# Projecting the next layer's first tile inside the last feed-forward groups, with separate buffers for W1's parts and another order in a feed-forward group (a linear-attention block, then a six-layer local-attention transformer, fp32, one core)

## Chip, cores and metric

One core of a Trainium2 chip. The metric is device time in microseconds; lower is better. Engines: TensorE (PE), VectorE (DVE), ScalarE (ACT), GpSimd (POOL), and SyncE (SP), whose queue here issues every DMA.

## What is computed

Input `x` is (4, 1024, 128). First a linear-attention block with 16 heads of 8 is added to it, then `L0_ffn`, which is itself a stack of six layers of local attention (16 heads of 64, window 32) and a gated feed-forward:

```python
x = x + _L0_attn_ref(_layernorm(x), Wq, bq, Wk, bk, Wv, bv, Wo, bo)
x = x + _L0_ffn_ref(_layernorm(x), ...)          # the six layers:
for i in range(6):
    x = attn_layer(shift_tokens(x), Wqkv[i], q_scale[i], k_scale[i], Wo[i]) + x
    x = ffn_layer(shift_tokens(x), ln_g[i], ln_b[i], W1[i], b1[i], W2[i], b2[i]) + x
# attn_layer: q, k l2-normed per head, scaled, rotary, softmax over own and previous window, @ Wo
# ffn_layer: xn = layernorm(x) * g + b; a, gate = split(xn @ W1 + b1); a * gelu(gate) @ W2 + b2
```

`shift_tokens` takes the second half of the channels from the token before. 4096 tokens are 32 tiles of 128 (`NT`), and 8 groups of 4 tiles (`NG`, `FT`) in the feed-forward.

## The kernel before

All five engines have their own instruction stream, written out by hand; they meet at semaphores (`wait_ge`, `then_inc`). Within an engine everything runs in the order of its text. For tile semaphores `done(T)` is the count after tile (or group) T.

**Attention of a layer.** `every_tile(step, depth)` runs `step(k)` for each tile as a software pipeline: step k holds the projection of tile k (`project`, three matmuls of 512 columns per half, from a high and a low part of `x` and of `Wqk`), the transposes, scores and value products of tile k-1, and the outputs of tiles k-2 and k-3. For one tile: TensorE transposes it (`xs_transposed`), ScalarE copies its high part (`xsT_upper`), DVE makes the low part (`xsT_lower`), TensorE projects `q` and later `k`; ScalarE squares them (`square`), DVE multiplies by the rotary tables (`rotate`) and makes the norms (`inverse_norms`), GpSimd adds (`add_rotated`, line 1545) and scales `k` (`normalise_k`, line 1554), TensorE transposes the results (line 595). Value and output weights are multiplied into `wvo` once per layer (`wv_transposed`, `wvo_product` on TensorE; `wvT_evacuated`, `wvo_evacuated` on ScalarE); the high and low part of `Wqk` are made by `wqk_upper` (ScalarE) and `wqk_lower` (GpSimd), in two pieces of 811 and 1237 columns.

**Feed-forward of a layer.** Eight groups. For group u, from the SP queue's `ffn_tokens(u)` (three DMAs: 128 partitions, 127 partitions, 1 partition) into one of six buffers `xs4`: DVE `centre` (lines 768, 770), ScalarE `squared4`, DVE `variance4` (line 775 on), GpSimd `group_rsqrt` (12 steps, lines 1457 to 1460), DVE `normalised` (line 785, writes `xn4`), TensorE `transpose4` (line 506), ScalarE `transposed` and `upper`, DVE `lower` (line 1111). Then TensorE `up(u, par, 0..2)` (lines 526 to 528), ScalarE `gelu`, DVE `hidden`, TensorE `down` (line 540), DVE `x_new` (line 1128) with `xb` that GpSimd's `x_and_bias` made (line 1569). Within `step4` DVE runs `hidden(u,1)`, `hidden(u,2)`, `normalised(u+2)`, `centre(u+3)`, `hidden(u+1,0)`, `variance4(u+3)`, `lower(u+2)`, `x_new(u)`. `W1`'s parts and `xnT`'s parts lie in `wqk_hi` and `wqk_lo`, which the attention no longer needs; so `w1_upper` (ScalarE) and `w1_lower` (GpSimd) run at the end of the attention, and the two pieces of the next layer's `wqk_upper` wait until the `up` of group 6 and of group 7 are through.

**SP queue.** In order: `ffn_tokens` 2 to 5, the next layer's attention weights (4 DMAs, 2 MB), `ffn_tokens` 6 and 7, the next layer's first two tiles.

**Between layers** TensorE runs, behind the last `up`: `wvo_product` 0, half of `down(7)`, `wvo_product` 1, the other half, `wvo_product` 2 and 3, then `step(0)` of the next layer. At the very end DVE adds the kept first sum (`x_keep`) for four batches and SP writes four outputs.

## Time and profile before

| | us |
|---|---|
| median of 3 runs | 3455.31 (3452.45 to 3456.94) |
| the profiled execution | 3454.96 |
| its span, first to last instruction | 3453.1 |

```profile
DVE  7788888678888668888768888877888866888876
ACT  3399998579999759999849999867999975999994
PEclk8799999999999999999999999999999999999999
```

The three lines are the span in 40 equal slices, with the busy share of VectorE and of ScalarE in tenths, and the TensorE clock that was granted, in tenths of full speed. A layer is about 550 us, 460 of them attention. In the sections below a row of a timeline is: start, length (us), engine, line, operation, output<-inputs, count, and in brackets the idle time of the engine before it with what ended it. Matmuls overlap: each is issued before the one ahead has ended. A row of a table of stages is: from:to, length, then busy time of each engine with its count of instructions, granted TensorE clock, DMA share, GB/s.

### The profile page before, as it was taken

Reading aid. Unit: us, or ns where it says so; the run is one execution under the profiler, and the core shown is the slowest. Engines: PE = TensorE matmul, PEld = TensorE weight load, DVE = VectorE, ACT = ScalarE, POOL = GpSimd, SP = SyncE. Lnnn points to the kernel's source line nnn. Section 1 sums busy time; section 2 is a strip of 40 time slices with the busy share of each in tenths; the row PEclk is TensorE's granted clock in tenths of the full one; section 3 lists DMA queues with packets and bytes.
Section 4 is the critical chain, followed back from the end, with each engine's and each line's share of the span. In section 5 each row is a group of like instructions: output and inputs, shape, how many; then the busy total and the mean of one; then the engine's idle time right before and its main releaser. Section 6 shows DMA issues by size and latency. Waiting matters only on the chain.

```text
span 3453.1 us, 114079 instructions
## 1 busy us (share of the span) xinstructions
PE 3204.9 (93%) x42076; PEld 2183.8 (63%) x42076; DVE 2797.3 (81%) x5376; ACT 2928.4 (85%) x9250; POOL 2035.8 (59%) x2150
## 2 busy tenths in 40 slices
PE   5699999889999889999889999988999988999997
PEld 4466666756666666666566666565666666666666
DVE  7788888678888668888768888877888866888876
ACT  3399998579999759999849999867999975999994
POOL 3466665456666556666556666555666655666654
PEclk8799999999999999999999999999999999999999
DMA  2000000100000100000010000010000010000002
GB/s 72 10 7 7 13 7 5 45 14 7 14 7 6 43 15 7 12 9 7 11 46 7 7 13 7 5 46 14 7 13 7 7 40 17 8 9 11 7 9 65
DMA packets 141016, 57.20 MB, mean 17 GB/s; under 512 B 118598, under 2 KB 137668, under 8 KB 139460
## 3 DMA queue, kind: packets, MB, share of 16 engines
q1 hardware_dynamic: 140484, 50.01, 6.2%
q8 instruction: 346, 5.67, 0.7%
q14 instruction: 186, 1.52, 0.1%
HBM read 22.57 MB, written 2.10 MB: 7 GB/s over the span
## 4 chain that ended last, share of the span: by engine, by line
PE 66%; DVE 11%; ACT 11%; POOL 6%; issue 5%; DVEq 0%; DMA 0%; SPq 0%; ACTq 0%; POOLq 0%
PE ring L649 16%; PE ring L595 9%; PE ring L667 7%; PE s_ps L633 7%; ACT probs L1341 6%; PE qk_ps L581 5%; PE ring L607 4%; PE qk_ps L582 4%; PE qk_ps L583 4%; PE s_ps L637 2%; DVE xn L785 2%; PE s_ps L624 2%; PE ring L540 1%; POOL qk_rot L1554 1%; POOL ln_rs L1458 1%
## 5 line engine op out<-in xcount | busy, mean ns | idle before, releaser
L1341 ACT ACTIVATE probs<-s_ps,nbias,rnorm 128x64 f32<-128x64 f32 x3072 | 1234.3, 450 | 0.4 <-DVE nbias L1060 0.4
L1545 POOL TENSOR_TENSOR qk_rot<-by_cos,by_sin 128x1024 f32<-128x1024 f32 x384 | 912.1, 2376 | 362.0 <-DVE by_sin L1010 318.9
L649 PE MATMUL ring<-wvo,xsT 128*32 128x512 f32 x6144 | 801.7, 605 | 18.1 <-ACT vo L1164 17.9
L1341 ACT ACTIVATION_READ_ACCUMULATOR probs<-s_ps,nbias,rnorm 128x1 f32 x3072 | 771.3, 251 | 0.0
L1534 POOL TENSOR_TENSOR probs<-probs,rrow 128x256 f32<-128x256 f32 x768 | 454.7, 613 | 309.6 <-DVE rrow L994 308.8
L1554 POOL TENSOR_TENSOR qk_rot<-qk_rot,rnorm 128x1024 f32<-128x1024 f32 x192 | 365.5, 1904 | 416.8 <-DVE rnorm L752 416.8
L1007 DVE TENSOR_TENSOR by_cos<-qk_ps,rotary 128x1024 f32<-128x1024 f32 x378 | 462.9, 1225 | 156.8 <-ACT squares L1327 156.4
L595 PEld LDWEIGHTS ring<-cst,qk_rot 128*128 128x128 f32 x3072 | 343.9, 141 | 279.3 <-ACT vo L1164 145.3
L595 PE MATMUL ring<-cst,qk_rot 128*128 128x128 f32 x3072 | 448.4, 279 | 75.9 <-POOL qk_rot L1545 51.7
L1022 DVE TENSOR_REDUCE sumsq<-squares 128x16 f32<-128x1024 f32 x384 | 463.2, 1206 | 0.0
L1010 DVE TENSOR_TENSOR by_sin<-qk_ps,rotary 128x1024 f32<-128x1024 f32 x378 | 459.3, 1215 | 0.0
L1327 ACT ACTIVATE squares<-qk_ps 128x1024 f32<-128x1024 f32 x378 | 399.4, 1057 | 40.0 <-PE qk_ps L583 40.0
L633 PE MATMUL s_ps<-kT,qT 128*32 128x128 f32 x10752 | 421.9, 279 | 0.0
L667 PEld LDWEIGHTS ring<-vo,pT 128*32 128x32 f32 x12288 | 344.6, 110 | 117.7 <-issue 117.7
L667 PE MATMUL ring<-vo,pT 128*32 128x128 f32 x12288 | 372.5, 273 | 5.0 <-ACT pT L1164 5.0
L1164 ACT ACTIVATE kT<-ring 64x512 f32<-64x512 f32 x576 | 339.5, 589 | 43.9 <-PE ring L595 35.1
L581 PE MATMUL qk_ps<-wqk_hi,xsT_hi 128*128 128x512 f32 x756 | 342.8, 453 | 5.2 <-DVE xsT_lo L984 5.1
L1164 ACT ACTIVATE vo<-ring 128x512 f32<-128x512 f32 x576 | 326.0, 602 | 8.2 <-PE ring L649 2.3
L633 PEld LDWEIGHTS s_ps<-kT,qT 128*32 128x32 f32 x10752 | 283.7, 109 | 60.9 <-issue 60.7
L649 PEld LDWEIGHTS ring<-wvo,xsT 128*32 128x32 f32 x6144 | 158.1, 110 | 249.3 <-ACT vo L1164 163.7
L582 PE MATMUL qk_ps<-wqk_lo,xsT_hi 128*128 128x512 f32 x756 | 304.8, 403 | 0.0
L583 PE MATMUL qk_ps<-wqk_hi,xsT_lo 128*128 128x512 f32 x756 | 304.4, 403 | 0.0
(173 smaller groups left out, 5372.8 us busy)
## 6 DMA issues: line engine op xcount, KB each, us to landing
qk_rot<-L_ffn_Wqkv SPq DMA_DIRECT2D x7, 1024.0 KB, 5.2
xs<-x_tok SPq DMA_DIRECT2D x194, 32.0 KB
xs<-x_tok SPq DMA_DIRECT2D x194, 31.8 KB
wv<-L_ffn_Wqkv SPq DMA_DIRECT2D x7, 512.0 KB, 6.8
wo_pad<-L_ffn_Wo SPq DMA_DIRECT2D x14, 256.0 KB, 7.8
xs<-x_tok SPq DMA_DIRECT2D x194, 0.2 KB
xs_first<-x_tok SPq DMA_DIRECT2D x24, 128.0 KB
by_cos<-x_tok SPq DMA_DIRECT2D x24, 128.0 KB
```

Of the source, the lines that this page charges most:

```text
L581: mm(half, xsT_hi[:, a, :], wqk_hi[:, cols], start=True, stop=False)
L595: last = nc.tensor.transpose(r[:, p * P:(p + 1) * P], qk_rot[:, 1 if qk == "k" else 0, c:c + P], ident)
L633: last = mm(sc, q, keys[:, :, c:c + 2 * WIN], start=False, stop=True, skip_group_check=True)
L649: last = mm(r[WIN * mh:WIN * (mh + 1), :], xsT[:, a, WIN * w:WIN * (w + 1)], wvo[:, mh, :, :], start=True, stop=True)
L667: last = mm(r[WIN * w:WIN * (w + 1), 0:C], pT[:, quad, side, WIN * w:WIN * (w + 1)], vo[:, at_w, quad * C:(quad + 1) * C], start=(n == 0), ...
L1007: v.tensor_tensor(heads(by_cos[:, n, :]), heads(projection_banks(qk, k, s)), table.unsqueeze(1).broadcast_to([P, H, D]), ALU.mult)
L1010: last = v.tensor_tensor(halves(by_sin[:, n, :])[:, :, ::-1, :], halves(projection_banks(qk, k, s)), table.rearrange("p (x j) -> p x j", x ...
L1022: v.tensor_reduce(sumsq[:, n * H:(n + 1) * H], heads(squares[:, n * INNER:(n + 1) * INNER]), AX, ALU.add).then_inc(summed[qk], 1)
L1164: return nc.scalar.activation(out_, in_, ACT.Copy)
L1341: last = nc.scalar.activation(probs[:, a, h // 4, :, h % 4, :], s_ps[:, half, c:c + 2 * WIN].rearrange("p (s c) -> p s c", s=2), ACT.Exp, ...
L1534: last = g.tensor_tensor(p, p, r, ALU.mult)
L1545: g.tensor_tensor(qk_rot[:, n, :], by_cos[:, n, :], by_sin[:, n, :], ALU.add).then_inc(added[qk], 1)
```

## The change

- `W1`'s two parts get buffers `w1_hi` and `w1_lo` of their own. `w1_upper` moves from behind the attention to ahead of ScalarE's step NT-6, `w1_lower` from ahead of GpSimd's step NT to ahead of NT-4.
- `xs4`'s first two buffers now lie in `hid`. Group 6 uses the buffer of group 2, group 7 that of group 3; group 6 is fetched ahead of the next layer's weights, group 7 still behind them.
- In `step4` DVE runs `centre(u+3)` ahead of `normalised(u+2)` and `variance4(u+3)` ahead of `hidden(u+1,0)`; ScalarE runs `squared4(u+3)` ahead of `gelu(u+1,0)`. GpSimd waits for `xn` of group u+2 before `x_and_bias(u)`, for u = 0 to 3.
- The tile-0 work of layers 1 to 5 moves into the layer before: transpose and `q` projection ahead of `down(7)`, the `k` projection between `wvo_product` 1 and 2, with the ScalarE and DVE parts that belong to it. `down(7)` is no longer cut by `wvo_product`. `wqk_upper` and `wqk_lower` now take two pieces of 1024 columns, the first of them during the groups. `wvo_product` uses banks 2, 3, 2, 3.
- The last layer no longer prepares weights for a layer that doesn't come. Three of the four final sums go to GpSimd, in its last groups.

The diff, cut to its changed lines (indentation reduced):

```diff
@@ -148,6 +148,7 @@
 w1 = sb("w1", [P, W1_COLS])
+w1_hi, w1_lo = [sb(name, [P, W1_COLS], F32R) for name in ("w1_hi", "w1_lo")]
@@ -178,7 +179,6 @@
 xn4 = sb("xn4", [P, FT, C])
-xs4_first = sb("xs4_first", [P, 2, FT * C])
@@ -187,13 +187,12 @@
 xs4_late = by_cos[:, :, :].rearrange("p a (b n) -> p (a b) n", b=2)
-xs4 = [(xs4_first[:, i, :] if i < 2 else xs4_late[:, i - 2, :]).rearrange("p (t c) -> p t c", t=FT) for i in range(6)]
+xs4 = [(hid[:, i + 1, :] if i < 2 else xs4_late[:, i - 2, :]).rearrange("p (t c) -> p t c", t=FT) for i in range(6)]
...
-late = 2 * INNER - W1_COLS - FT * P
-w1_hi, w1_lo = [parts[:, late:late + W1_COLS] for parts in (wqk_hi, wqk_lo)]
-xnT_hi, xnT_lo = [[parts[:, c:c + FT * P] for c in (late - FT * P, late + W1_COLS)]
+late = INNER
+xnT_hi, xnT_lo = [[parts[:, c:c + FT * P] for c in (late, late + FT * P)]
@@ -284,9 +283,11 @@
 def xs4_buffer(u):
-    return u % 6
...
-wvo_banks = (0, 0, 2, 3)
+    return u if u < 6 else u - 4
...
+def wvo_bank(r, layer):
...
+    return (2, 3, 2, 3)[r] if layer else (0, 0, 2, 3)[r]
@@ -385,7 +386,7 @@
         for p in (2 * r, 2 * r + 1):
-            last = mm(ring[:, wvo_banks[r], (p % 2) * 2 * C:(p % 2 + 1) * 2 * C], wvT[:, p, :], wo_pad[:, p, :, :],
+            last = mm(ring[:, wvo_bank(r, layer), (p % 2) * 2 * C:(p % 2 + 1) * 2 * C], wvT[:, p, :], wo_pad[:, p, :, :],
@@ -478,6 +479,7 @@
         pe.wait_ge(wq_ready, 2 * l + 2)
+        last_layer = l == DEPTH - 1
@@ -669,6 +671,17 @@
                 last.then_inc(o_ps, 1)
+            if only == "queries":
+                xs_transposed(0)
+                project("q", 0, 0)
+                project("q", 1, 0)
+                return
+            if only == "keys":
+                project("k", 0, 0)
+                project("k", 1, 0)
+                return
+            if k == 0 and l > 0:
+                return
@@ -717,18 +730,27 @@
         pe.wait_ge(g_xnT, done(NG * l + NG - 1))
-        wv_transposed(0, l + 1)
+        if not last_layer:
+            wv_transposed(0, l + 1)
...
-        pe.wait_ge(wvT_ready, 2 * l + 3)
-        wv_transposed(1, l + 1)
+        if not last_layer:
+            pe.wait_ge(wvT_ready, 2 * l + 3)
+            wv_transposed(1, l + 1)
...
-        wvo_product(0, l + 1)
-        down(NG - 1, 1, 0, FT // 2)
-        wvo_product(1, l + 1)
-        down(NG - 1, 1, FT // 2, FT)
-        for r in range(2, WVO_ROUNDS):
-            wvo_product(r, l + 1)
+        if not last_layer:
+            pe.wait_ge(wvT_ready, 2 * l + 4)
+            pe.wait_ge(wq_ready, 2 * l + 3)
+            pe.wait_ge(g_hid, passed(3 * (NG * l + NG - 1) + 1))
+            step(0, l + 1, "queries")
+        down(NG - 1, 1)
+        if not last_layer:
+            wvo_product(0, l + 1)
+            wvo_product(1, l + 1)
+            pe.wait_ge(wq_ready, 2 * l + 4)
+            step(0, l + 1, "keys")
+            wvo_product(2, l + 1)
+            wvo_product(3, l + 1)
@@ -925,7 +947,7 @@
             b = xs4_buffer(u)
-            dve.wait_ge(g_xs[b], 48 * (l * (2 if b < NG - 6 else 1) + u // 6) + 48)
+            dve.wait_ge(g_xs[b], 48 * (l * (2 if b in (2, 3) else 1) + u // 6) + 48)
@@ -947,7 +969,7 @@
             scaled(xs4[xs4_buffer(u)], xn4[:, :, :], ln_rs[:, par, 2, :], counted, norm_g).then_inc(g_xn, 1)
-        def step(k):
+        def step(k, l=l, only=None):
@@ -1068,7 +1090,10 @@
                 v.tensor_tensor(x_old, ring[:, ring_bank(a, "o"), 0:C], x_old, ALU.add).then_inc(x_mid, 1)
-            xsT_lower(0)
+            if k or l == 0 or only == "lower":
+                xsT_lower(0)
+            if only == "lower":
+                return
@@ -1132,16 +1157,18 @@
             hidden(u, par, 2)
+            if ahead3:
+                centre(u + 3, 1 - par)
...
-                centre(u + 3, 1 - par)
+                variance4(u + 3, 1 - par)
...
-            if ahead3:
-                variance4(u + 3, 1 - par)
...
+            if u == NG - 1 and l < DEPTH - 1:
+                step(0, l + 1, "lower")
@@ -1153,9 +1180,8 @@
     dve.wait_ge(x_ready, NT * (DEPTH + 1))
-    for b in range(B):
-        tiles = x_keep[:, b * TPB:(b + 1) * TPB, :]
-        v.tensor_tensor(tiles, tiles, x_cols(b * TPB, TPB), ALU.add).then_inc(final_ready, 1)
+    tiles = x_keep[:, (B - 1) * TPB:B * TPB, :]
+    v.tensor_tensor(tiles, tiles, x_cols((B - 1) * TPB, TPB), ALU.add).then_inc(last_ready, 1)
@@ -1175,7 +1201,7 @@
         act.wait_ge(wvo_ps, WVO_ROUNDS * layer + r + 1)
-        copy(wvo[:, :, r, :], ring[:, wvo_banks[r], :].rearrange("p (a c) -> p a c", a=4)).then_inc(wvo_ready, 1)
+        copy(wvo[:, :, r, :], ring[:, wvo_bank(r, layer), :].rearrange("p (a c) -> p a c", a=4)).then_inc(wvo_ready, 1)
@@ -1257,7 +1283,7 @@
     for l in range(DEPTH):
-        def step(k):
+        def step(k, l=l, only=None):
@@ -1346,6 +1372,18 @@
                     last.then_inc(exp_done[half], 1)
+            if only == "upper":
+                xsT_upper(0)
+                return
+            if only == "queries":
+                xsT_evacuated(0)
+                square("q", 0)
+                return
+            if only == "keys":
+                square("k", 0)
+                return
+            if k == 0 and l > 0:
+                return
@@ -1402,17 +1440,15 @@
             act.wait_ge(w1_in, 16 * l + 16)
-            act.wait_ge(projected["k"], done(NT * l + NT - 1))
-            copy(w1_hi, w1[:, :]).then_inc(w1_hi_ready, 1)
+            copy(w1_hi[:, :], w1[:, :]).then_inc(w1_hi_ready, 1)
...
-            w1_upper()
...
-        every_tile(step, 2, {NT + 1: first_group})
+        every_tile(step, 2, {NT - 6: w1_upper, NT + 1: first_group})
@@ -1421,26 +1457,34 @@
             gelu(u, 2)
-            gelu(u + 1, 0)
...
+            gelu(u + 1, 0)
...
-        wvT_evacuated(0, l + 1)
-        act.wait_ge(g_up, passed(6 * (NG * l + NG - 1)))
-        wqk_upper(l + 1, 0)
+            if u == 4 and l < DEPTH - 1:
+                wqk_upper(l + 1, 0)
+        if l < DEPTH - 1:
+            wvT_evacuated(0, l + 1)
...
-        wvT_evacuated(1, l + 1)
+        if l < DEPTH - 1:
+            wvT_evacuated(1, l + 1)
...
-        wvo_evacuated(0, l + 1)
-        act.wait_ge(g_up, passed(6 * (NG * l + NG)))
-        wqk_upper(l + 1, 1)
-        for r in range(1, WVO_ROUNDS):
-            wvo_evacuated(r, l + 1)
+        if l < DEPTH - 1:
+            step(0, l + 1, "upper")
+            act.wait_ge(g_up, passed(6 * (NG * l + NG)))
+            wqk_upper(l + 1, 1)
+            act.wait_ge(g_down, done(NG * l + NG - 1))
+            step(0, l + 1, "queries")
+            wvo_evacuated(0, l + 1)
+            wvo_evacuated(1, l + 1)
+            step(0, l + 1, "keys")
+            wvo_evacuated(2, l + 1)
+            wvo_evacuated(3, l + 1)
@@ -1569,6 +1613,12 @@
                             b2_row[:, :].unsqueeze(1).broadcast_to([P, FT, C]), ALU.add).then_inc(g_xb, 1)
+        def final_sum(b):
...
+            tiles = x_keep[:, b * TPB:(b + 1) * TPB, :]
+            pool.wait_ge(x_ready, NT * DEPTH + (b + 1) * TPB)
+            g.tensor_tensor(tiles, tiles, x_cols(b * TPB, TPB), ALU.add).then_inc(final_ready, 1)
@@ -1582,24 +1632,32 @@
             pool.wait_ge(w1_hi_ready, l + 1)
-            g.tensor_tensor(w1_lo, w1[:, :], w1_hi.bitcast(F32), ALU.subtract).then_inc(w1_ready, 1)
...
-        every_tile(step, 1, {NT - 2: first_rsqrts, NT: w1_lower})
+            g.tensor_tensor(w1_lo[:, :], w1[:, :], w1_hi[:, :].bitcast(F32), ALU.subtract).then_inc(w1_ready, 1)
...
+        every_tile(step, 1, {NT - 4: w1_lower, NT - 2: first_rsqrts})
...
+            pool.wait_ge(g_xn, done(NG * l + u + 2))
...
-        tables(l + 1)
+        if l < DEPTH - 1:
+            wqk_lower(l + 1, 0)
+            tables(l + 1)
+        else:
+            final_sum(0)
+            final_sum(1)
...
+        if l == DEPTH - 1:
+            final_sum(2)
...
-        for part in range(2):
-            wqk_lower(l + 1, part)
+        if l < DEPTH - 1:
+            wqk_lower(l + 1, 1)
@@ -1681,9 +1739,9 @@
         load(b2_row[:, :], row(b2[layer, :].rearrange("l n -> (l n)")), b2_in)
-        after = (l + 1) % DEPTH
-        sp.wait_ge(tables_ready, l + 1)
-        scales(after)
+        if l < DEPTH - 1:
+            sp.wait_ge(tables_ready, l + 1)
+            scales(l + 1)
@@ -1692,7 +1750,7 @@
             if u < 2 or u >= 6:
-                buffer_read = ahead(sp, done(NG * l + u - (2 if u < 2 else 6)))
+                buffer_read = ahead(sp, done(NG * l + u - (2 if u < 2 else 4)))
@@ -1714,23 +1772,27 @@
         last_tile = done(NT * l + NT - 1)
-        for u in range(2, 6):
+        for u in range(2, 7):
...
-        for half in range(2):
-            sp.wait_ge(qT_ps[half], last_tile)
-            sp.wait_ge(kT_ps[half], last_tile)
-        for w in range(NW):
-            sp.wait_ge(vo_ps[w], last_tile)
-        attention_weights(after)
-        for u in range(6, NG):
-            ffn_tokens(u)
...
-        for a in range(2):
-            attention_tokens(l + 1, a, a, NT * l + NT + FT)
+        if l < DEPTH - 1:
+            for half in range(2):
+                sp.wait_ge(qT_ps[half], last_tile)
+                sp.wait_ge(kT_ps[half], last_tile)
+            for w in range(NW):
+                sp.wait_ge(vo_ps[w], last_tile)
+            attention_weights(l + 1)
+        ffn_tokens(NG - 1)
...
+        if l < DEPTH - 1:
+            for a in range(2):
+                attention_tokens(l + 1, a, a, NT * l + NT + FT)
...
-        sp.wait_ge(xs_in[a], 24 * NT * DEPTH + 48)
+        sp.wait_ge(xs_in[a], 24 * NT * DEPTH)
...
-        sp.wait_ge(final_ready, b + 1)
+        if b < B - 1:
+            sp.wait_ge(final_ready, b + 1)
+        else:
+            sp.wait_ge(last_ready, 1)
```

## Rows read from the trace of the kernel before

**Rows 1.** The page's first part: busy us, share of the span, instructions.

```profile
PE 3204.9 (93%) x42076; PEld 2183.8 (63%) x42076; DVE 2797.3 (81%) x5376; ACT 2928.4 (85%) x9250; POOL 2035.8 (59%) x2150
```

**Rows 2.** Table of stages: an attention tile, feed-forward groups, the transition.

```profile
1057.90:1071.80 13.90, 13.90 (x207) 9.09 (x202) 12.12 (x25) 13.74 (x47) 8.99 (x7) 1.00 0.04 8
...
634.30:677.80 43.50, 37.95 (x234) 32.25 (x232) 35.04 (x54) 19.91 (x32) 22.60 (x67) 1.00 0.26 67
...
690.00:722.00 32.00, 24.48 (x181) 16.25 (x179) 19.52 (x29) 13.91 (x23) 12.99 (x6) 0.84 0.12 27
```

**Rows 3.** Waits in 633 to 690: who for whom, sum, times, longest.

```profile
PE ring L506 <- DVE xn L785: 5.6, 5, 1.1
```

**Rows 4.** Timelines of the engines in one feed-forward group, and `normalised` in attention.

```profile
634.29 0.47 PE L526 MATMUL s_ps<-wqk_hi 128*128 128x512 f32 x1
...
636.73 0.69 ACT L1399 ACTIVATE by_sin<-ring,b_col 85x512 f32<-85x512 f32 x1 [0.35 <-PE ring L528]
...
639.55 0.61 PE L540 MATMUL ring<-w,hid 128*128 128x128 f32 x4
641.26 0.63 PE L506 MATMUL ring<-cst,xn 128*128 128x128 f32 x4 [1.11 <-DVE xn L785]
...
639.30 1.26 POOL L1569 TENSOR_TENSOR xb<-x_tok,b_row 128x512 f32<-128x512 f32 x1
...
639.46 1.66 DVE L785 TENSOR_TENSOR xn<-by_cos,ln_rs 128x512 f32<-128x512 f32 x1 [1.02 <-POOL ln_rs L1460]
641.04 0.67 DVE L768 TENSOR_REDUCE ln_rs<-by_cos 128x4 f32<-128x512 f32 x1
...
611.75 0.69 DVE L785 TENSOR_TENSOR xn<-xs_first,ln_rs 128x512 f32<-128x512 f32 x1
```

**Rows 5.** Timeline of the SP queue in the first layer's feed-forward (the DMAs' issue).

```profile
607.15 32.65 SPq L1608 DMA_DIRECT2D by_cos<-x_tok  x12
...
643.15 20.17 SPq L1608 DMA_DIRECT2D xs_first<-x_tok  x6
```

**Rows 6.** DMA issues in 600 to 700: size, median us from issue to landing.

```profile
ln_col<-L_ffn_ln_g SPq DMA_DIRECT2D x1, 0.5 KB, 1.9
```

**Rows 7.** Timeline of TensorE from the first layer to the second.

```profile
688.41 1.02 PE L388 MATMUL ring<-wo_pad,wvT 128*128 128x256 f32 x4
...
698.02 0.76 PE L581 MATMUL qk_ps<-wqk_hi,xsT_hi 128*128 128x512 f32 x1 [0.85 <-DVE xsT_lo L984]
...
707.08 1.12 PE L595 MATMUL ring<-cst,qk_rot 128*128 128x128 f32 x4 [4.36 <-POOL qk_rot L1545]
...
714.34 0.63 PE L595 MATMUL ring<-cst,qk_rot 128*128 128x128 f32 x4 [0.24 <-POOL qk_rot L1554]
...
718.59 0.33 PE L564 MATMUL ring<-cst,xs 128*128 128x128 f32 x1
```

**Rows 8.** The same one layer on, where the first projections ran at full clock.

```profile
1248.35 0.47 PE L581 MATMUL qk_ps<-wqk_hi,xsT_hi 128*128 128x512 f32 x1 [0.85 <-DVE xsT_lo L984]
...
1267.65 0.33 PE L564 MATMUL ring<-cst,xs 128*128 128x128 f32 x1
```

**Rows 9.** Timelines: the two `w1` operations, then GpSimd and TensorE in the last attention tiles.

```profile
612.41 0.81 ACT L1164 ACTIVATE wqk_hi<-w 128x725 fp32r<-128x725 f32 x1
...
613.30 1.74 POOL L1585 TENSOR_TENSOR wqk_lo<-w,wqk_hi 128x725 fp32r<-128x725 f32 x1 [3.50 <-ACT wqk_hi L1164]
...
1100.04 2.37 POOL L1545 TENSOR_TENSOR qk_rot<-by_cos,by_sin 128x1024 f32<-128x1024 f32 x1 [0.35 <-issue]
...
1102.56 0.63 PE L595 MATMUL ring<-cst,qk_rot 128*128 128x128 f32 x4
...
1134.51 0.70 PE L595 MATMUL ring<-cst,qk_rot 128*128 128x128 f32 x4 [3.95 <-POOL qk_rot L1545]
```

**Rows 10.** Timeline of DVE at the end.

```profile
3442.24 4.63 DVE L1158 TENSOR_TENSOR x_keep<-x_keep,x_tok 128x1024 f32<-128x1024 f32 x4
```

**Rows 11.** The output's DMAs.

```profile
DMA to landing us min/median/max: 3.4/4.5/5.8
```

## Prediction before the run

> **What bounds the kernel now.** I read the page's busy shares first [rows 1], then a table of stages [rows 2], then the timeline of each engine at the places that the change touches. TensorE is busy 93% of the span, but the stages have different limits. In the attention loop a tile takes 13.9 us, TensorE is busy for all of it and ScalarE for 13.74 us [rows 2]: there a delay on either engine is paid in full. In the feed-forward stretch TensorE has 5.5 us free in 43.5, and in the stretch from one layer to the next 7.5 free in 32, at a granted clock of 0.84 [rows 2]. These two stretches can give something; the attention loop can only lose.
>
> **Feed-forward, groups 1 to 4.** What ends TensorE's wait in a group is the `xn` of two groups ahead: 1.11 us, five times a layer [rows 3]. The timeline of one group shows a ring that keeps itself going [rows 4]: GpSimd ends a reciprocal root at 639.3; DVE's `normalised` starts at 639.46 and lasts 1.66, since GpSimd's `x_and_bias` (639.30, 1.26) runs beside it, where the same operation with no GpSimd work beside it takes 0.69; then `centre` (0.67 and as much again), the squares, the variance, and GpSimd's twelve small steps. One round is 8.70 us. TensorE's work in it is 8.70 - 1.11 and, as matmuls overlap (the last four of the first half of `down` are issued from 639.55 at 0.11 each, so the transposes could go at 639.99 and go at 641.26), 8.70 - 1.27 = 7.43.
> The new order puts `centre(u+3)` ahead of `normalised(u+2)`, into the time in which DVE waits for GpSimd (1.02 [rows 4]), and holds `x_and_bias` until `xn` is written. Counted from the first `up` of a group (634.29 in the rows): the gate's last part is through at +3.13 and `hidden(u,2)` can start at +3.27. DVE is free 0.66 later, at +3.93; `centre` needs 0.71 + 0.61; `normalised` 0.69, at +5.25 to +5.94; the transposes start 0.14 behind it, +6.08. TensorE is there at +5.70 (639.99). So it waits 0.38 instead of 1.27, the round is 7.81, and a group gains 0.89. GpSimd keeps up: `x_and_bias` ends at 7.3, the variance's small steps are held until then as `normalised` is now, the root starts at 7.8 and takes 3.7, i.e. it is there at +3.7 of the next group, before `centre` ends. The first group gains 0.39 by the same count (`xn` at 632.04 instead of 632.42). In group 5 there is no `centre`, `normalised` can start at +3.93, and the whole 1.27 goes.
> The Trainium skill (SBUF — State Buffer, Who interferes with whom) says that a DVE operation with two SBUF inputs and a GpSimd operation that reads SBUF exclude each other for a whole instruction. The rows agree: 1.66 is the rest of 1.26 plus one operation.
>
> **What is late next: group 7's tokens.** The 12 transfers of groups 2 to 5 take the SP queue from 607.15 to 639.80, 8.15 us a group; then the weights' four are issued until 643.15; groups 6 and 7 take 20.17 (to 663.3), of which 12.1 are group 6's, behind the weights, if group 7 takes its 8.1 [rows 5]. The change puts group 6 ahead of the weights, but group 7 behind them. The queue has the same work up to group 7: 5 x 8.15 + 3.35 (weights) + 12.1 from 607.15, so its small last part is again issued at about 663.4. A small transfer lands 1.9 after its issue begins [rows 6]; this one's issue begins earlier and ends there, I take 1.6, so group 7 is there at about 665.0. Today `centre(7)` starts at 667.14 and doesn't see that. With groups of 7.81 it wants to start at 634.29 - 0.39 + 3 x 7.81 + 3.93 = 661.3. DVE then stands 3.7 us, and since `centre(7)` is now ahead of `normalised(6)`, TensorE stands too: transposes at 665.0 + 1.32 + 0.69 + 0.15 = 667.2, next group at 668.9, where it is at 669.09 now. Of what groups 0 to 4 gain (0.39 + 4 x 0.89 = 3.95) next to nothing is left, 0.16; with group 5's 1.27 a layer gains 1.4. In the last layer no weights are fetched any more, group 7 is there at about 658, and it gains the full 3.95 + 1.27 = 5.2. Together 5 x 1.4 + 5.2 = 12.3.
> The Trainium skill (DMA: Bandwidth & Descriptors, Why a DMA increments its semaphore by 16 and not by 1) says that a transfer over 127 partitions runs on one engine of 16. The trace agrees: 256 KB of tokens take 8.15 us and 2 MB of weights add about 4 to that and 2.6 for their issue. By the page nothing in the change makes these transfers shorter.
>
> **From one layer to the next, five times.** Now the last `up` ends at 688.41, `wvo` and `down` follow, both projections of the first tile run from 698.02 to 702.4, and then TensorE waits 4.36 for `q` (rotated on DVE, added on GpSimd) [rows 7]. `k`'s transposes start at 714.34, behind DVE's norms and GpSimd's product [rows 7]. New, worked out with the durations of these rows: transpose of the tile at 688.4; its upper part behind `gelu(7,2)` on ScalarE at 688.8, the lower part on DVE behind `hidden(7,2)` until 689.75; TensorE waits 1.1, projects `q` until 691.3, `down(7)` until 694.0, 0.6 later than now, on which only the next layer's loads wait. ScalarE waits for `down` (its squares' buffer is read by it), squares `q` until 695.35, evacuates `wvo` 0 until 695.9; TensorE `wvo` 1 until 696.9, then `k` until 698.3 (in `s_ps`), `wvo` 2, ScalarE the square of `k` until 699.4, `wvo` 3 is evacuated at 701.7. Tile 1's transpose then comes at 701.8 (702.45 now), `q`'s transposes at 702.0 (707.08), the next `q` projection at 703.0 (708.19). DVE rotates `k` until 701.8 (707.9), norms are through at 706.0, GpSimd's product at 708.0, `k`'s transposes start at 708.2 (714.34). The later of these chains sets the end: 6.1 us. Two of the five transitions are 1.27 shorter today, as the first projections run at full clock (19.30 from the first one to the third tile's transpose, where layer 1 takes 20.57 [rows 7, 8]); there I take 4.8. Sum 6.1 + 4.8 + 5.8 + 6.0 + 4.8 = 27.5. The waits left are short, so I take the full clock for the new matmuls; at the lower of its two levels, 1.2 instead of 2.4 GHz (0.43 apart instead of 0.23), `k`'s path would lose about 1.5 each time. Bounds 3 and 6.5 a transition. The wider `wqk_upper` on ScalarE (1.05) lies behind group 4, in a gap of 0.6 to 2 before the next gate part: nothing. GpSimd's `wqk_lower` and `tables` together need 8.3 between `x_and_bias` 5 and 6 and end at 681.6, before `x_new(6)` at 684: nothing, or 0.5 where they hold back the last `lower`.
>
> **Attention, a loss.** `w1_upper` now costs nothing: at 612.41 (0.81) it ends before the transposes that ScalarE needs next are through (613.22) [rows 9]. At tile NT-6 it is put before the work of a ScalarE that is full: +0.7. `w1_lower` (1.74 [rows 9]) is put ahead of GpSimd's `add_rotated("q")` of tile NT-4. That sum ends at 1102.41 (starts at 1100.04, 0.35 after GpSimd's last operation) and TensorE takes it at 1102.56 with no wait: no cover but the 0.35. So +1.4. The same place one step on shows what happens: there the first roots take GpSimd 4.1 us, and TensorE stands 3.95 [rows 9]. No later slack takes it back. Six layers: 6 x (0.7 + 1.4) = +12.6. Bounds for both: 0 and 2.5 a layer. `w1_hi`'s own buffer by itself changes no time; nor do the aliases of `xs4` in `hid`, which is idle then.
>
> **The end.** Layer 5 drops two transposes of `wv` (0.43, 0.35) and `wvo` 1 between the halves of `down` (0.87), so the last `x_new` starts at 3439.7, not 3441.5. Three of the four final sums go to GpSimd earlier; one (1.22) is left instead of 4.63 [rows 10], until 3441.6. The last output is then alone: 3.4 from issue to landing at the least [rows 11], so the end is at 3445.1, not 3453.1. 8.0.
>
> **Sum.** The profiled execution took 3454.96 (span 3453.1), 0.35 under the median 3455.31. -27.5 - 12.3 - 8.0 + 12.6 = -35.2: 3419.8, or 3420 on the median.
>
> **Rivals.**
> 1. Group 7 isn't late (its transfers shrink without the weights' share in front of them, or the small last part lands sooner). For it: the 12.1 of group 6 may be mostly waiting at the weights' issue. Against: group 6 met the same weights and took 12.1. Then 5 x 3.7 more: 3401.5. Chance 0.17.
> 2. `w1_lower` and `w1_upper` hide: 12.6 less, 3407; half of it 3413. For it: ScalarE has 0.16 free a tile. Against: the 3.95. Chance 0.13.
> 3. The transition gives only 3: TensorE's clock stays at the lower level, or the chain transpose, ScalarE, DVE, TensorE in it is longer. For it: 0.84 today, and four more short waits. 5 x 2.5 more: 3432. Chance 0.15.
> 4. Slower than before: group 7 lands still later, since its parts stand behind 2 MB of weights and `centre(7)` holds `normalised(6)`, `hidden(5,0)` and all behind it on DVE. Every us is paid by TensorE in five layers. 35.2 / 5 = 7 us, so landing after 672 instead of 665 decides; at 674 it would be 3465. For it: group 6 grew by 4 behind the weights. Against: I have counted those 4. Chance 0.03.
> 5. The new order doesn't do what it says: `normalised` stays at 1.66 or the round at 8.7, so that only transition, end and loss are left: 3420 + 12 = 3432. Against: with the wait nothing of GpSimd can run there. Chance 0.04.
>
> **How the numbers follow.** The forecast itself (3411 to 3429) gets 0.48, the rivals 0.52. The range takes in 1, 3 and 5 and leaves out both mechanisms together at either side: 3399 to 3436. About 0.2% (7 us) can be told from no change. All cases but the fourth, and sums of the third with a group 7 that is some us later, lie below 3448: faster 0.94, same 0.03, slower 0.03.
>
> **What would show it.** `normalised` at 0.69 in groups 2 to 5; TensorE's wait before the transposes near 0.4, but one of some 4 us a layer before group 6's, ended by a DMA, in layers 0 to 4 only; a new wait of TensorE of 1.4 at tile NT-3 for GpSimd's sum and a tile at NT-6 that is 0.7 longer; the distance from the last `up` of a layer to `k`'s transposes at 20 us instead of 26; one final sum on DVE and one output after it. Wrong would be: no DMA wait (then rival 1), or a layer period that falls by less than 3 us.

## The result, and the profile after

| | before | after |
|---|---|---|
| median (lowest to highest) | 3455.96 (3452.45 to 3456.94) | 3434.72 (3432.22 to 3438.57) |
| the profiled execution, its span | 3454.96, 3453.1 | 3438.57, 3436.7 |

The ratio is 0.9943, with an interval of 0.9930 to 0.9955. The change makes the kernel 0.6% faster, not 1.0%: between the two profiled executions 16.4 us are gained, where the sum had 35.2.

To see where, I cut both spans at four events that each layer has: the low part of tile 3 (DVE), the transposes of group 1 and of group 7 (TensorE, `xn`), and the low part of the next layer's tile 3. Summed over the layers, in us:

| stretch | before | after | difference | the sum had |
|---|---|---|---|---|
| tile 3 to group 1 (attention), 6 layers | 2588.9 | 2606.3 | +17.4 | +12.6 |
| group 1 to group 7, layers 0 to 4 | 288.3 | 293.4 | +5.1 | -7.1 |
| the same in layer 5 | 57.6 | 52.7 | -4.9 | -5.2 |
| group 7 to the next tile 3, 5 transitions | 303.5 | 276.5 | -27.0 | -27.5 |
| group 7 of layer 5 to the end | 29.1 | 22.1 | -7.0 | -8.0 |

The parts ahead of layer 0's tile 3 are equal. Of the 18.8 us that are missing, 12.2 are in the second row.

TensorE in the first layer's groups 5 to 6, kernel after. A row: start, length, engine, line, operation, output<-inputs, count, and in brackets the wait before it and what ended it.

```profile
657.32 0.63 PE L508 MATMUL ring<-cst,xn 128*128 128x128 f32 x4 [0.31 <-DVE xn L807]
...
669.95 1.09 PE L508 MATMUL ring<-cst,xn 128*128 128x128 f32 x4 [4.92 <-DVE xn L807]
670.83 2.77 PE L542 MATMUL ring<-w,hid 128*128 128x128 f32 x12
673.25 0.77 PE L528 MATMUL s_ps<-wqk_hi,w_hi 128*128 128x512 f32 x1
673.82 0.63 PE L529 MATMUL s_ps<-wqk_lo,w_hi 128*128 128x512 f32 x1
...
675.96 0.41 PE L528 MATMUL ring<-wqk_hi,w_hi 128*128 128x512 f32 x1
676.20 0.39 PE L529 MATMUL ring<-wqk_lo,w_hi 128*128 128x512 f32 x1
```

DVE and the SP queue in the same stretch, kernel after:

```profile
656.49 0.68 DVE L807 TENSOR_TENSOR xn<-by_cos,ln_rs 128x512 f32<-128x512 f32 x1
...
667.79 0.69 DVE L790 TENSOR_REDUCE ln_rs<-by_cos 128x4 f32<-128x512 f32 x1 [4.48 <-DMA by_cos<-x_tok]
...
608.96 41.19 SPq L1666 DMA_DIRECT2D by_cos<-x_tok  x15
...
654.43 11.20 SPq L1666 DMA_DIRECT2D by_cos<-x_tok  x3
...
657.01 8.62 SPq L1666 DMA_DIRECT2D by_cos<-x_tok  x1
```

(The last row is a part of the one above it: the issue of group 7's third transfer, of one partition, behind the one over 127 partitions.)

The wait of 1.11 that [rows 3] show is down to 0.31, and `normalised` takes 0.68, not 1.66 [rows 4]. But `centre(7)` stands 4.48 for its DMA, and behind it TensorE 4.92. Then come slow matmuls: the four transposes 1.09 instead of 0.63, the products 0.43 apart instead of 0.23, until 676. The line on what the reading of the tokens in `centre` (L790) waited for gives the five waits of DVE together, 4.48, 3.81, 3.56, 2.55 and 3.95 us in layers 0 to 4 (sum, number):

```profile
  DMA by_cos<-x_tok: 18.3, 5
```

Table of stages, kernel after: seven us behind that wait in layers 0 to 4 (from:to, length, busy time of PE, PEld, DVE, ACT, POOL, the granted TensorE clock, DMA share, GB/s).

```profile
669.00:676.00 7.00, 6.05 (x23) 5.50 (x24) 3.90 (x8) 4.25 (x6) 4.01 (x14) 0.51 0.05 10
1218.00:1225.00 7.00, 6.47 (x30) 5.93 (x31) 4.23 (x8) 4.93 (x7) 4.14 (x14) 0.76 0.05 10
1764.00:1771.00 7.00, 6.46 (x30) 5.87 (x31) 4.25 (x8) 4.81 (x7) 4.42 (x14) 0.76 0.06 12
2311.00:2318.00 7.00, 6.28 (x24) 5.68 (x25) 3.67 (x7) 4.25 (x6) 4.24 (x14) 0.52 0.05 11
2862.00:2869.00 7.00, 6.87 (x28) 6.20 (x29) 3.85 (x7) 3.99 (x7) 4.83 (x14) 0.62 0.03 6
```

A share of 1.00 is 2.4 GHz, and 0.50 is 1.2 GHz. So 0.51 to 0.76 means that TensorE ran at 1.2 GHz for about half to nearly all of the seven us. What it did before was to stand for 2.9 to 4.9 us.

The transition is as worked out. TensorE, kernel after, to be held against [rows 7]:

```profile
692.15 0.39 PE L530 MATMUL ring<-wqk_hi,w_lo 128*128 128x512 f32 x1
692.38 0.27 PE L566 MATMUL ring<-cst,xs 128*128 128x128 f32 x1
693.85 0.47 PE L583 MATMUL qk_ps<-wqk_hi,xsT_hi 128*128 128x512 f32 x1 [1.20 <-DVE xsT_lo L1006]
...
706.12 0.60 PE L597 MATMUL ring<-cst,qk_rot 128*128 128x128 f32 x4
...
712.50 0.63 PE L597 MATMUL ring<-cst,qk_rot 128*128 128x128 f32 x4 [1.13 <-POOL qk_rot L1598]
```

From the start of the last `up` matmul to `k`'s transposes it is 20.34 to 20.69 us in the five transitions, where before it was 26.2 in this one (688.17 to 714.34). The wait of 4.36 for `q` is gone.

### The profile page after: what moved, and what is told of

Its sections match the earlier page's. It is cut to its first block, busy times and chain, and to the rows that moved or that the text cites. A ratio compares the mean times of both kernels' runs of the same rounds, so it can differ in the third digit from the quotient of the medians.

```text
span 3436.7 us, 114006 instructions
## 1 busy us (share of the span) xinstructions
PE 3199.3 (93%) x42052; PEld 2184.7 (64%) x42052; DVE 2762.4 (80%) x5373; ACT 2926.4 (85%) x9242; POOL 2035.2 (59%) x2147
## 4 chain that ended last, share of the span: by engine, by line
PE 67%; ACT 8%; DVE 8%; SPq 6%; issue 4%; POOL 4%; DMA 2%; DVEq 0%; POOLq 0%; ACTq 0%
PE ring L651 16%; PE ring L597 9%; PE ring L669 7%; PE s_ps L635 7%; SPq L1666 6%; PE qk_ps L583 5%; PE qk_ps L584 4%; PE qk_ps L585 4%; PE ring L609 4%; ACT probs L1367 4%; PE s_ps L639 2%; PE ring L542 2%; PE s_ps L626 2%; DMA by_cos<-x_tok 2%; POOL qk_rot L1598 1%
## 5 line engine op out<-in xcount | busy, mean ns | idle before, releaser
L1071 DVE TENSOR_REDUCE smax<-s_ps 128x8 f32<-128x512 f32 x384 | 261.1, 680 | 56.4 <-PE s_ps L635 56.4
```

## The experiments

All are edits of the changed kernel; each name stands again at its result below. The median is that of all executions, the stretches are those of the table above, read from the profiled execution, in us:

| run | median | attention | groups, 0 to 4 | groups, 5 | transitions | end |
|---|---|---|---|---|---|---|
| after | 3434.7 | 2606.3 | 293.4 | 52.7 | 276.5 | 22.1 |
| e1_g7_first | 3406.4 | 2605.2 | 262.7 | 53.0 | 273.3 | 22.0 |
| e2_split | 3406.9 | 2604.3 | 263.0 | 53.0 | 277.5 | 22.0 |
| e12_filler | 3428.6 | 2608.0 | 281.5 | 52.8 | 276.8 | 22.0 |
| e5_old_order | 3436.1 | 2603.4 | 288.3 | 57.6 | 276.6 | 22.5 |
| e6_no_hold | 3412.3 | 2607.3 | 265.6 | 53.1 | 276.6 | 22.0 |
| e3_w1_back | 3414.9 | 2589.1 | 290.8 | 52.8 | 270.7 | 22.0 |
| e8_early | 3399.8 | 2593.3 | 262.5 | 54.0 | 277.5 | 22.0 |
| e9_back_g7 | 3396.6 | 2591.6 | 265.2 | 54.0 | 274.6 | 22.1 |
| e4_no_move | 3473.2 | 2604.2 | 292.8 | 52.1 | 314.4 | 22.0 |
| e13_old_tail | 3464.4 | 2606.4 | 288.1 | 52.8 | 304.4 | 22.0 |
| e7_dve_sums | 3435.5 | 2607.3 | 289.4 | 52.1 | 272.1 | 27.0 |

(Groups, 0 to 4 and groups, 5: from group 1's to group 7's transposes in these layers.)

### Group 7 ahead of the weights

```diff
-for u in range(2, 7):
+for u in range(2, NG):
     ffn_tokens(u)
 ...
     attention_weights(l + 1)
-ffn_tokens(NG - 1)
```

> The changed kernel with one edit: group 7 is fetched ahead of the next layer's weights, like group 6. Theory L (group 7 is late behind the weights): from the transposes of group 1's successor (xn of group 1) to those of group 7 the changed kernel takes 59.82, 58.17, 57.56, 58.56 and 59.29 us in layers 0 to 4 and 52.66 in layer 5, which fetches no weights. Without the wait all take 52.7: 30.1 us less, 3434.7 - 30 = about 3405 (3402 to 3409), no DMA wait of DVE before centre(7), and a granted clock of 1.00 where it was 0.51. Rival W (the wait only moves): the weights are now issued some 8 us later, ScalarE's first piece of the weights or the transposes of wv stand instead, and less than half of the 30 us is gained: 3420 to 3435.

Measured (e1_g7_first): 3406.35; the ratio to the kernel before is 0.9856 (0.9839 to 0.9872). The groups of layers 0 to 4 take 262.7, 30.7 less, and the other stretches keep their times within 3.2 us. The weights, now issued from 659.39, make nothing wait. So group 7's place in the queue alone cost the changed kernel 28 us, 1.3 times what the whole change brought.

### The 127-partition transfer cut in two

```diff
-dve.wait_ge(g_xs[b], 48 * (l * (2 if b in (2, 3) else 1) + u // 6) + 48)
+dve.wait_ge(g_xs[b], 64 * (l * (2 if b in (2, 3) else 1) + u // 6) + 64)
 ...
-load(xs4[b][1:P, :, hi], here[0:P - 1, :, hi], g_xs[b])
+load(xs4[b][1:113, :, hi], here[0:112, :, hi], g_xs[b])
+load(xs4[b][113:P, :, hi], here[112:P - 1, :, hi], g_xs[b])
```

> The changed kernel, group 7 still behind the weights, but the 127-partition transfer of each group's shifted half is cut into one of 112 and one of 15 partitions. Theory E (the 127 partitions go over one of the 16 DMA engines, and that sets the 8.15 us a group): a group takes under 3 us of the queue, group 7 is there long before 660, and the same 28 us are gained as by fetching it ahead of the weights: 3406 (3402 to 3411). Rival Q (the queue's time goes by descriptors, not by engines): a group still takes 8 us or a little more, group 7 is as late: 3433 to 3440.

Measured (e2_split): 3406.89, the same gain with group 7 still behind the weights. The SP queue in that kernel:

```profile
609.68 28.25 SPq L1666 DMA_DIRECT2D by_cos<-x_tok  x20
638.25 0.35 SPq L1666 DMA_DIRECT2D qk_rot<-L_ffn_Wqkv  x1
...
642.42 3.27 SPq L1666 DMA_DIRECT2D by_cos<-x_tok  x4
```

Group 7's issue takes 3.27 for four transfers instead of 11.20 for three, behind the same 2 MB. (The 28.25 of the five groups ahead of them hold 11 us in which the queue waits for group 6's buffer.) What is gone is the 8.62 for which the issue of the one-partition transfer stood behind the 127-partition one; it takes 0.70 now. The bytes and the number of pieces are the same, so it was the width of the transfer that held the queue. The two kernels together say that the weights by themselves don't delay group 7; only a slow transfer behind them did.

### The wait kept, its pause filled

```diff
     pe.wait_ge(g_xnT, done(U - 1))
+    if u == NG - 2 and not last_layer:
+        for _ in range(13):
+            mm(ring[:, 0, :], w1_hi[:, 0:P], w1_hi[:, 0:FT * P], start=True, stop=True)
     pe.wait_ge(g_xn, done(U))
```

> The changed kernel, group 7 as late as ever, but in layers 0 to 4 TensorE runs 13 matmuls of 512 columns (0.23 us each, 3.0 together) on W1's high part, whose result nobody reads, in the time in which it waits for xn of group 6 (2.94 to 4.92 us). The DMA wait stays. Theory C (behind the wait the granted clock is 0.51 until 676, and that alone makes the stretch from group 6's transposes to group 7's 9.74 us on average instead of 7.31): the stretch is 7.3 to 7.8 again, 5 x 2.4 = 12.2 less at the most: 3422.5 (3421 to 3428). Rival (other engines' queues, held up by the wait, set that stretch): it stays at 9 to 10 and the time at 3433 to 3437.

Measured (e12_filler): 3428.55, and the stretch from group 6's transposes to group 7's is 7.33 to 7.34 in all five layers (10.15, 9.50, 9.11, 10.17, 9.76 in the changed kernel). TensorE and the granted clock, kernel with the filler:

```profile
666.85 3.21 PE L508 MATMUL ring<-w_hi 128*128 128x512 f32 x13
672.18 0.66 PE L511 MATMUL ring<-cst,xn 128*128 128x128 f32 x4 [2.12 <-DVE xn L810]
672.67 1.50 PE L545 MATMUL ring<-w,hid 128*128 128x128 f32 x12
...
671.00:678.00 7.00, 5.82 (x34) 5.03 (x34) 5.70 (x11) 5.08 (x8) 3.69 (x13) 1.00 0.06 11
```

`xn` comes as late as before (DVE's five waits for the DMA are 18.4 us together, 18.3 without the filler); only TensorE's pause is shorter, 2.12, 0.52, 0.32, 1.56 and 0.56 us in layers 0 to 4, and the clock is 1.00 in the seven us behind it in all five, where it was 0.51 to 0.76. The groups of layers 0 to 4 take 11.9 less. That is what the lower clock cost, by itself. The total fell by 6 to 8 only, just short of my range, since the attention stretch was 1.7 longer and the start of layer 0 some 2 us, where the clock varies too (below).

### The old order in a group, and GpSimd's hold

Both on top of group 7 ahead of the weights. The first puts `normalised` ahead of `centre`, `variance4` behind `hidden(u+1,0)`, `squared4` behind `gelu(u+1,0)`, and takes the hold away; the second takes only the hold away:

```diff
 for u in range(NG - 4):
-    pool.wait_ge(g_xn, done(NG * l + u + 2))
     x_and_bias(u)
```

> The first of these kernels (group 7 ahead of the weights) with the old order in a feed-forward group on DVE and ScalarE and without GpSimd's wait for xn. Theory O (the order sets the round, 7.77 against 8.70 us, in groups 1 to 5): 4.93 us a layer more than the first kernel, six layers, 29.6: about 3435, normalised at 1.66 us and TensorE's wait at 1.1 again. Rival P (once group 7 is in time the round is set by TensorE and the order matters little): under 12 us more, below 3417.

> Group 7 ahead of the weights, new order on DVE and ScalarE, but GpSimd doesn't wait for xn before x_and_bias. Measured without this edit: 3406.35, round 7.77. Theory H (the 1.26 us of x_and_bias then run beside centre's second operation and push normalised): round about 8.15, 30 groups x 0.35, some 10 us more: 3416 (3411 to 3424). Rival N (centre ahead of normalised is enough, the hold isn't needed): 3404 to 3409.

Measured: 3436.14 (e5_old_order) and 3412.33 (e6_no_hold). The old order gives back 29.8 us: a group takes 8.70 again, a layer 57.6 to 57.9 instead of 52.1 to 53.1. That is, the new order with its hold was worth 5.0 a layer, and in layers 0 to 4 of the changed kernel group 7 took all of it back. Without the hold alone the median is 6.0 higher, but not as I had expected: the round stays at 7.77, and `x_and_bias` runs beside `centre` in the first round of a layer only. GpSimd, DVE and TensorE without the hold:

```profile
632.52 1.26 POOL L1613 TENSOR_TENSOR xb<-x_tok,b_row 128x512 f32<-128x512 f32 x1
...
632.67 1.66 DVE L792 SCALAR_TENSOR_TENSOR by_cos<-ln_rs,by_cos 128x512 f32<-128x512 f32 x1
...
635.08 0.63 PE L508 MATMUL ring<-cst,xn 128*128 128x128 f32 x4 [1.28 <-DVE xn L807]
```

With the hold that operation takes 0.69, TensorE's wait is 0.31, and the stretch from group 1's to group 2's transposes 13.72 instead of 14.68. It does so in layers 0, 2 and 4 only; in the other three the granted clock is lower in this stretch (0.88 instead of 1.00), it takes 14.6 with the hold as well, and 14.7 without it. The spans of the two profiled executions are 7.8 apart. Of these 3.0 lie in the groups, where the hold acts; 2.1 lie in the attention and 3.3 in the transitions, where it changes nothing, and the start of layer 0 is 0.5 shorter. Theory H named the collision and had its count wrong: once a layer, not in each of five rounds; its time came about by the rest.

### W1's parts elsewhere

Back behind the attention tiles, in buffers of their own; in the second tile of a layer (with group 7 ahead of the weights); and back, with group 7 ahead:

```diff
-every_tile(step, 2, {NT - 6: w1_upper, NT + 1: first_group})   # ScalarE
-every_tile(step, 1, {NT - 4: w1_lower, NT - 2: first_rsqrts})  # GpSimd
+every_tile(step, 2, {NT + 1: first_group})                     # with w1_upper() first in it
+every_tile(step, 1, {NT - 2: first_rsqrts, NT: w1_lower})
```

> The changed kernel with the making of W1's two parts moved back behind the attention tiles (ScalarE at the first group, GpSimd at tile 32), their own buffers kept. Theory A (the two operations lengthen two tiles by 0.6 and 1.28 us in each layer and nothing takes it back): 6 x 1.9 = 11.3 us less, about 3423.5 (3421 to 3427), and tiles 26 and 29 back at 13.9. Rival B (group 7's tokens set the end of the feed-forward in layers 0 to 4 whenever the attention ends): their fetch starts with the end of the attention, so it moves with it and the gain stays; if instead it were tied to something else, layers 0 to 4 would give nothing and only layer 5 1.9: 3433.

> Group 7 ahead of the weights, and W1's parts made in the second tile of the layer, where the changed kernel's trace shows ScalarE idle for 2.85 us and then GpSimd for 2.75 (layer 0 to 1, from 710.35 and 712.35); their own buffers allow it. Theory G (both hide there): tiles 26 and 29 are 13.9 again, 11.3 us less than 3406.35, and with the clock that was lower after the 1.28 us stand up to 6 more: 3391 (3387 to 3396), under both kernels. Rival (GpSimd's 1.74 delays tile 2's sum as it did at tile 29): 1.3 to 1.7 a layer come back: 3399 to 3404.

> The changed kernel with both single edits: group 7 ahead of the weights, W1's parts made behind the attention tiles. Alone they gave 28.4 and 19.8 us, of the second 11.3 by the two tiles and the rest in stretches where TensorE's clock was higher. Theory (they add up): 3406.35 - 11.3 = 3395, down to 3387 where the clock's part comes too. Rival (the clock's part went because group 7's lateness gave TensorE a rest, so it doesn't add): 3395 to 3400, no better than making the parts in the second tile.

Measured: 3414.89 (e3_w1_back), 3399.83 (e8_early) and 3396.58 (e9_back_g7; 3390.67 to 3407.66, ratio 0.9837, 0.9814 to 0.9859). From low part to low part, tile 25 to 26 takes 14.51 in the changed kernel and tile 29 to 30 about 15.20 (the expectations call them tiles 26 and 29; in layer 2 a third of a us of the second lies one tile earlier), in every layer; in all three of these kernels both take 13.9: 6 x (0.60 + 1.28) = 11.3. The first kernel gained 19.8 by the medians, where I had forecast 11.3. Its profiled execution gained 25.3: 17.2 in the attention, 5.8 in the transitions, 2.6 in the groups. What goes beyond the 11.3 lies in stretches that have the same work, and another clock (below). The parts made in the first tiles gave their 12.0 in the attention, but the total is 8.8 above my 3391, in the range of the rival. The rival's mechanism is there in one layer of six. GpSimd's 1.77 lay one step later than I had meant. In layer 1 it filled an idle 1.5 ahead of a sum that came 0.2 later, and in layers 1 to 5 the step from tile 3 to 4 is no more than 0.12 longer. In layer 0 TensorE waits 1.43 for that sum, and from tile 2 to 4 it takes 1.6 longer. The transitions took 277.5 instead of 273.3, with a lower clock at tile 2 (16.68 and 17.84 where it had been 15.14 and 15.15). The last kernel has the lowest median and beats both the kernel before, by 1.6%, and the changed one, by 1.1%; from the second of these three, whose times lie inside its own, it can't be told. The two single gains add, as far as they come from waits; the part of the clock did not come along.

### The transition

First without the move of tile 0, then with the old tail besides:

```diff
-    step(0, l + 1, "queries")     # and "keys", on TensorE and ScalarE; "upper"; "lower" on DVE
 ...
+    wvo_product(0, l + 1)         # the second kernel only; banks 0, 0, 2, 3
+    down(NG - 1, 1, 0, FT // 2)
+    wvo_product(1, l + 1)
+    down(NG - 1, 1, FT // 2, FT)
```

> The changed kernel without its move of tile 0: transpose, both projections, squares and the low part of the next layer's first tile are again in that layer's own first step; all else stays (banks 2, 3, 2, 3 and whole down(7) too). From the transposes of group 7 to the start of tile 3's low part the kernel before takes 61.3, 59.95, 60.97, 61.23, 60.0, the changed one 55.32, 53.75, 56.47, 55.64, 55.28. Theory T (the move alone gives this): 27 us more, about 3461 (3456 to 3465). Rival (a good part comes from the other bank order and the whole down(7), which stay): under 15 us more, 3435 to 3450.

> The changed kernel without the move of tile 0, as in the third kernel, and besides with the old tail: down(7) cut in two halves with wvo 0 and 1 ahead of them, banks 0, 0, 2, 3, ScalarE's evacuation of wvo 0 ahead of the second piece of the weights. Five transitions took 303.5 us in the kernel before, 276.5 in the changed one and 314.4 in the third kernel, where TensorE waited 1.11 for down(7) and 0.69 to 0.75 before each wvo product. Theory D (the uncut down costs 2.2 a transition when nothing else fills the waits): 303 again, 11 less than the third kernel's 3473: 3462 (3459 to 3466). Rival (the larger second piece of the weights or the buffers cost it): 310 to 315, 3469 to 3475.

Measured: 3473.22 (e4_no_move; I had forecast 3461) and 3464.35 (e13_old_tail). Without the move the transitions take 314.4, 10.9 more than before the change. TensorE, kernel without the move:

```profile
694.15 0.46 PE L542 MATMUL ring<-w,squares 128*128 128x128 f32 x2 [1.11 <-DVE hid L1139]
...
698.68 1.13 PE L389 MATMUL ring<-wo_pad,wvT 128*128 128x256 f32 x4 [0.75 <-ACT wvo L1182]
700.50 1.13 PE L389 MATMUL ring<-wo_pad,wvT 128*128 128x256 f32 x4 [0.69 <-ACT wvo L1182]
702.32 1.13 PE L389 MATMUL ring<-wo_pad,wvT 128*128 128x256 f32 x4 [0.69 <-ACT wvo L1182]
```

With the old tail it is 304.4, against 303.5 before. So on top of the new tail the move is worth 38 us, and the new tail without the move costs 10 to 11; the package gives 27. The tail is three things at once: `down(7)` uncut, the banks 2, 3, 2, 3, and ScalarE's copy of `wvo` 0 behind the second piece of the weights. Which of them costs the 10 wasn't run by itself; the waits of 1.11 and 0.69 to 0.75 above, against 0.24 and 0.69 before the change, come to 2.3 a transition. My forecast had the sum right by its own path, but never priced the tail without the move.

### The final sums

On DVE again, as before:

> The changed kernel with all four final sums on DVE again, behind the last x_new. Read from the transposes of group 7 to the end of the span: 29.09 us before, 22.07 in the changed kernel. Theory S (three sums of 1.14 each and outputs that queue behind each other): 5.4 more, 27.5, and 1.6 of the 7.0 are the missing transposes of wv. Rival (GpSimd's sums delay the last groups by what they save): 22 to 24. The total would be about 3440.

Measured (e7_dve_sums): the end takes 26.96 instead of 22.07, i.e. the sums on GpSimd bring 4.9 of the 7.0. The total, 3435.5 in one execution, doesn't show it: the transitions were 4.4 and the groups 4.0 shorter there. A single total of this kernel can't tell 5 us; the stretch can, since the end varies by 0.1 (one kernel: 0.5) between all others.

## Why the prediction was wrong

**Feed-forward, layers 0 to 4: -7.1 forecast, +5.1 measured.** The step that failed is "transposes at ... 667.2, next group at 668.9". Its first half held. The attention's loss shifts all by 1.8 here: from group 1's to group 6's transposes a layer takes 48.94 on average, 48.96 before, and I had put 48.8. The wait is ended by the DMA, in layers 0 to 4 only, and on average of the length said (3.7; 18.3 / 5 = 3.66), though the single ones go from 2.55 to 4.48 and layer 0, which I had worked out, is the longest. The second half was wrong. I let TensorE go on at the speed of [rows 4] after having stood; it went on at the lower clock. From group 6's to group 7's transposes it takes 9.74 on average, against the 7.43 of my sum and 7.31 where nothing waits: 5 x 2.31 = 11.5 of the 12.2. The term that I had put at nothing is what TensorE loses behind the wait. The filler takes the lower clock away and leaves the wait, and the stretch is 7.34 again. I had the row for it: the profile before shows projections at half speed behind a stand [rows 7], and I priced it for the transition as a rival and not for the wait that I added myself. That 3434.7 still lies inside 3399 to 3436 is luck: the range reached that high for rivals 3 and 5, and neither occurred.

**Rival 1** (group 7 isn't late) did not occur, but the runs with group 7 ahead or cut in two say what it would have given: 28 us less, where I had put 5 x 3.7 = 18.5. Here too the clock was left out of the price. The rule about 127 partitions, which I named beside this step (the Trainium skill, DMA: Bandwidth & Descriptors, Why a DMA increments its semaphore by 16 and not by 1), agrees with the cut into 112 and 15: 3.27 instead of 11.20.

**Attention: +12.6 forecast, +17.4 measured.** The mechanism and its two places were right: 0.60 and 1.28 a layer against 0.7 and 1.4, 11.3 in all. Kernel after, layer 1: GpSimd's `w1_lower` ahead of the sum, and TensorE's wait for that sum:

```profile
1098.27 1.77 POOL L1635 TENSOR_TENSOR w_lo<-w,w_hi 128x725 fp32r<-128x725 f32 x1
...
1102.50 0.63 PE L597 MATMUL ring<-cst,qk_rot 128*128 128x128 f32 x4 [1.17 <-POOL qk_rot L1589]
```

The other 6.1 lie outside these two waits. In two layers the step from tile 27 to 28 takes 17.4 to 17.5 instead of 15.86 (in the kernel before once, in layer 0), in three layers the stretch from tile 31 to group 1's transposes takes 38.0 to 38.4 instead of 37.1, together some 5 us, and in both cases the granted clock is lower (0.90 for 1.00 over the step, and 0.84 for 0.92 over the first 21 us of the stretch). That doesn't look like chance alone: in the nine kernels with `W1`'s parts in these tiles the attention takes 2603.4 to 2608.0, in the four without (the kernel before among them) 2588.9 to 2593.3. The averages are 15.1 apart, so some 4 us more than the two waits go with this edit. By what way is open.

**Transitions: -27.5 forecast, -27.0 measured**, by the path that was worked out (20.35 us against 20). **Layer 5** gained 4.9 of 5.2. **The end** gave 7.0 of 8.0: the last `x_new` comes 1.0 sooner after group 7's transposes, not 1.8, as TensorE waits 1.11 for `hid` ahead of `down(7)`.

**Rival 4** had the right price for one step ("every us is paid by TensorE"), but 1 us of waiting cost 1.6 on average here (29.9 us for 18.3, against five layers of 52.7), so it would have decided at a landing earlier than the 672 that I gave. **Rivals 2 and 3** did not occur, nor did 5: the order does what it says (the round is 7.77, where I had 7.81), the hold being needed in one round of a layer only.

## What to carry to other kernels

When a change makes the bottleneck engine wait in a place where it didn't, price the wait and what the engine loses behind it: here a stand of 3 to 5 us of TensorE was followed by 3 to 7 us at half the clock, 2.4 us lost each time on average. Where the wait itself can't be removed, work that nobody needs, put into it, gave these 2.4 us back. A transfer that is moved in a queue is to be costed with what stands ahead of it and with how many engines it spreads over; moving one fetch by one place in the queue was worth more than the whole change. And the order that shortened the loop by 5.0 us a layer showed none of it in the five layers in which one input of the loop was late.

## What the runs showed of the hardware that I had not expected

The same wait can be followed by either clock. In tile 2 of layers 1 to 5 TensorE stands 2.85 us for ScalarE. Kernel after, the eight us around the end of this wait in layer 2 and in layer 3, then tile 27 to 28 in layers 3 and 4:

```profile
1272.00:1280.00 8.00, 5.44 (x62) 3.77 (x63) 6.17 (x9) 7.92 (x25) 6.05 (x6) 1.00 0.00 0
1817.80:1825.80 8.00, 5.63 (x20) 3.28 (x21) 4.96 (x6) 5.54 (x21) 4.23 (x5) 0.60 0.01 2
...
2165.36:2181.21 15.85, 13.95 (x218) 9.21 (x213) 14.82 (x33) 13.79 (x47) 8.99 (x7) 1.00 0.02 5
2713.19:2730.61 17.42, 15.51 (x217) 10.34 (x208) 15.01 (x33) 13.84 (x47) 8.98 (x7) 0.90 0.03 6
```

Tile 2 to 3 takes 15.14 in the one case and 17.87 in the other (16.7 in the other three layers), tile 27 to 28 15.85 and 17.42, with the same instructions. Which case comes varies from layer to layer, and between executions of one kernel: the four of the last kernel had spans of 3388.5, 3393.9, 3395.2 and 3405.6 at mean granted clocks of 0.984, 0.980, 0.980 and 0.975. So each layer has several places that are worth 1 to 2.7 us by the clock alone.

Counted over all thirteen profiles: the stand of 2.85 at tile 2 was followed by the full clock in 13 of 65 cases and by a lower one in 52; the stand of 1.5 at the same place in layer 0 by the full clock in 13 of 13. In the five kernels in which group 7 is late and nothing fills the wait, 24 of 25 stands were followed by the lower clock. But the length of the stand alone doesn't decide: 1.92 us was followed by it (layer 1 with `W1`'s parts back, groups 6 to 7 in 9.55), 3.07 us was not (layer 0 with the old tail, 7.29), nor were the 0.32 to 2.12 us behind the filler. What decides between the cases I haven't settled.
